# Transposing x for a small attention: TensorE transposes and a ScalarE copy, or VectorE's block transpose and DMAs

## The chip, the cores and the metric

One Trainium2 chip, one of its cores. The metric is the device time of one launch of the kernel in microseconds (us), the median of several runs. Everything is computed in float32. TensorE's clock has two levels, 1.2 and 2.4 GHz; the profile shows the granted clock as a share of the higher one.

## The reference, cut to what matters

The program is a decoder of two layers on x of 4 x 1024 x 512. Six residual blocks follow each other, each ended by a layer norm. The change lies between the last two: a cross-attention onto every sixteenth key of a context of 64 (4 keys a head, 16 heads), and a gated feed-forward on values rounded block by block.

```python
    def _L1_xattn_ref(hidden_states, key_value_states, Wq, bq, Wk, bk, Wv, bv, Wo, bo, stride):
        ...
        Q = (hidden_states @ Wq.T + bq).reshape(B, Tq, H, D).transpose(0, 2, 1, 3)
        ...
        scores = jnp.einsum('bhqd,bhkd->bhqk', Q, Kg) * scaling
        attn = jax.nn.softmax(scores, axis=-1)
        out = jnp.einsum('bhqk,bhkd->bhqd', attn, Vg)
    ...
        gate = fp4_linear(x, w_gate)
        y = fp4_linear(x, w_up)
        h = jax.nn.silu(gate) * y
        return fp4_linear(h, w_down)
```

## The kernel before, in words

The last stage of the program, `attention_outputs_and_feed_forward`, takes x as 32 tiles (`NT`) of 128 rows by 512 features. Tile n passes through these steps, each with its engine and line:

- `local_out` (TensorE, L2054): the output product of the attention before. VectorE adds it to x (`local_sum`, L2251 to L2258) and normalises the tile (`local_normal`, L2263), four slots ahead of the tile's feed-forward. Tiles 0 to 2 had this done in the stage before.
- `transpose_x` (TensorE, L2062): four 128x128 transposes of the normalised tile into one PSUM bank, `bank[SCORES]`; `copy_x` (ScalarE, L2173) copies them to `tl_XT`, of which there are two, one for even and one for odd tiles. Each 128x128 chunk lies there contiguously.
- `scores` (TensorE, L2072): four matmuls a tile, with a chunk of `tl_XT` as the stationary operand (128 columns) and 64 columns of the folded query-key weights `tl_MQ` moving. Two tiles fill one softmax.
- `shifted`, `exp`, `weights` (VectorE, ScalarE, VectorE): the softmax of both tiles. `transpose_weights` (L2078) and `attend` (L2086) are TensorE's again.
- `attended_sum`, `attended_normal`, `x_quant` (VectorE): the residual, the norm and the rounding. `xq_turned` (L2381) is VectorE's transpose in blocks of 32x32; `xq_moved` then moves the 16 blocks of 32x128 from `tl_QB` to `tl_XQT` with 16 DMAs, 8 from SyncE's queue and 8 from ScalarE's (`blocks_moved`, L1986).
- `gate_and_up` (TensorE, L2099 and L2104), in three pieces of 512, 512 and 384 columns, with `tl_XQT` stationary; `silu` (ScalarE, L2179), `product` and the rounding of h (VectorE, L2341 to L2375), `h_turned` (L2385) and `h_moved` (again 8 + 8 DMAs), `down` (TensorE, L2116, 11 matmuls), `out_sum` and `out_normal` (VectorE, L2233 to L2245) and the store (SyncE, L2020).

In `tl_XQT` and `tl_HT` the elements of a chunk do not lie side by side: `chunk(x, c)` reads every fourth (or every eleventh) float of a partition. In `tl_XT` and in the operands of L2054 and L2137 they do lie side by side.

Each engine's program is a loop over slots s = -2 to 34. Slot s does gate and up of tile s, down of tile s-1, the store of tile s-2, and `local_out` of tile s+4. In even slots the pair of tiles s+2 and s+3 passes through `transpose_x`, `scores` and the softmax (`pair(s)`). Each engine and each DMA queue works strictly in the order written, with waits on semaphores in between. A matmul in float32 shows in the trace as two records, each with its own weight load: four matmuls are 8 records. Slots -1 and 0 are the filling.

Of the kernel before, what the change touches and what calls it, by code (L numbers as in the profile page):

```python
# [10 lines left out]
ACT = mybir.ActivationFunctionType  # L11
AX = mybir.AxisListType

P = 128
B = 4
T = 1024
D = 512
C = D // P
# [40 lines left out]
class Kernel:  # L59
# [25 lines left out]
    def sb(self, ctx, name, shape, dt=F32):  # L85
        return ctx.enter_context(self.nc.sbuf_tensor(name, shape, dt))
# [26 lines left out]
    def x_tile(self, b, g):  # L113
        return self.X[:, bass.ds(b * G * D + g * D, D)]
# [90 lines left out]
EARLY = 3  # L205
# [1704 lines left out]
def attention_outputs_and_feed_forward(k):  # L1910


    a, bank = k.a, k.bank
    HM = H * KPH
    NT = B * G
    DOWN, VOUT, LOUT, SCORES = 3, (4, 5), 6, 7
    QUANT = 9
    with ExitStack() as ctx:
        sb = lambda n, s, dt=F32: k.sb(ctx, "tl_" + n, s, dt)
        sem = lambda n: k.tick("tl_" + n)  # L1920
# [22 lines left out]
        s_fq, s_ft, s_fc = (sem(n) for n in ("first_xq", "first_xqT_mm", "first_xqT"))  # L1943

        assert 2 * HM == P and B % 2 == 0
        XT, PT, SM = [sb(f"XT{p}", [P, C, P]) for p in range(2)], sb("PT", [P, P]), sb("SM", [P, 2 * HM])
        mx, sm, rc = (sb(n, [P, 2 * H]) for n in ("mx", "sm", "rc"))
        st4, mv4, ve4, rs4 = sb("st4", [P, 6]), [sb(f"mv4{p}", [P, 2]) for p in range(2)], sb("ve4", [P, 1]), sb("rs4", [P, 1])
        st5, mv5, ve5, rs5 = sb("st5", [P, 6]), [sb(f"mv5{p}", [P, 2]) for p in range(2)], sb("ve5", [P, 1]), sb("rs5", [P, 1])
# [2 lines left out]


        XB, XQB = sb("XB", [P, D]), sb("QB", [P, D])
        tmp = sb("tmp", [P, FI])

        HQ = [sb(f"HQ{p}", [P, FI]) for p in range(2)]
# [10 lines left out]
        there = lambda n: 0 <= n < NT  # L1968

        pair = lambda s: s // 2 + 1 if s % 2 == 0 and there(s + 2) else None  # L1970

        LT = NT - 1
        by_blocks = lambda n: 0 <= n < LT
# [27 lines left out]
        with k.nc.Block() as block:  # L2001
            @block.sync
            def _(e):

                def load_attended(n):
                    b, g = n % B, n // B
                    e.wait_ge(s_lo.sem, s_lo.at(n - EARLY - 1))
                    for d in k.d_ao:
                        e.wait_ge(d, 16 * B * C)
                    e.dma_start(AT[n % 2][:, :, :], k.AOd[:, b * C:(b + 1) * C, g * P:(g + 1) * P]).then_inc(s_at[n % 2].sem, 16)  # L2010

                e.dma_start(MQ[:, :], k.SW[:, M2_AT:VO_AT]).then_inc(s_wm.sem, 16)
                load_attended(EARLY)
                load_attended(EARLY + 1)

                for s in SLOTS:
                    if there(s - 2):
                        n = s - 2
                        e.wait_ge(s_x6.sem, s_x6.at(n + 1))
                        e.dma_start(k.out[n % B, (n // B) * P:(n // B + 1) * P, :], x_tile(n)).then_inc(s_out.sem, 16)  # L2020
                    if by_blocks(s - 1):
                        h_moved(e, s - 1, (0, 1))
                    if 0 < s + 1 < NT:
                        xq_moved(e, s + 1, (0, 1))
                    if EARLY + 2 <= s + 6 < NT:
                        load_attended(s + 6)
                e.wait_ge(s_out.sem, s_out.at(16 * NT))
# [21 lines left out]
            def _(e):  # L2049
# [5 lines left out]
                    mm.then_inc(s_lo.sem, 1)  # L2055

                def transpose_x(n):
                    e.wait_ge(s_x4.sem, s_x4.at(n + 1 - EARLY))
                    e.wait_ge(s_tc.sem, s_tc.at(n))
                    e.wait_ge(s_pc.sem, s_pc.at(n // 2))  # L2060
                    for c in range(C):
                        mm = e.transpose(bank[SCORES][:, c * P:(c + 1) * P], x_tile(n)[:, c * P:(c + 1) * P], k.ident[:, :])  # L2062
                    mm.then_inc(s_t.sem, 1)

                def scores(n):
                    if n == 0:
                        e.wait_ge(s_wm.sem, s_wm.at(16))

                    e.wait_ge(s_tc.sem, s_tc.at(n // 2 * 2 + 2))
                    b = n % B  # L2070
                    for c in range(C):
                        mm = e.matmul(bank[SCORES][:, HM * (n % 2):HM * (n % 2) + HM], XT[n % 2][:, c, :], M2[:, c, b * HM:(b + 1) * HM],  # L2072
                                      start=(c == 0), stop=(c == C - 1))
                    mm.then_inc(s_s.sem, 1)

# [63 lines left out]

                for s in SLOTS:  # L2140
                    j = pair(s)
                    if j is not None:
                        transpose_x(2 * j)
                    if there(s):
                        gate_and_up(s, 0)
                    if j is not None:
                        transpose_x(2 * j + 1)
                    if there(s):
                        gate_and_up(s, 1)
                    if j is not None:  # L2150
                        scores(2 * j)
                        scores(2 * j + 1)
                    if later(s + 4):
                        local_out(s + 4)
                    if there(s):
                        gate_and_up(s, 2)
                    if s + 1 == 0:
                        first_turned()
                    if j is not None:
                        transpose_weights(j)  # L2160
                    if by_blocks(s - 1):
                        down(s - 1)
                    if s - 1 == LT:
                        last_down()
                    if j is not None:
                        attend(j)

            @block.scalar
            def _(e):
                def copy_x(n):  # L2170
                    e.wait_ge(s_t.sem, s_t.at(n + 1))
                    e.wait_ge(s_s.sem, s_s.at(n - 1))
                    e.activation(XT[n % 2][:, :, :], bank[SCORES][:, :].rearrange("p (c t) -> p c t", c=C), ACT.Copy).then_inc(s_tc.sem, 1)  # L2173

                def silu(n, q):
                    x, w = PIECES[q]
                    e.wait_ge(s_g.sem, s_g.at(NP * n + q + 1))
                    e.wait_ge(s_ht.sem, s_ht.at(n - 1))
                    e.activation(HQ[n % 2][:, x:x + w], bank[(2 * q) % 3][:, 0:w], ACT.Silu).then_inc(s_sg.sem, 1)  # L2179

                def exp(j):
                    e.wait_ge(s_sx.sem, s_sx.at(j + 1))
                    e.activation(SM[:, :], SM[:, :], ACT.Exp).then_inc(s_ex.sem, 1)

                def copy_weights(j):
                    e.wait_ge(s_pm.sem, s_pm.at(j + 1))
                    e.wait_ge(s_v.sem, s_v.at(2 * j))
                    e.activation(PT[:, :], bank[SCORES][:, P:2 * P], ACT.Copy).then_inc(s_pc.sem, 1)

                def first_copied():  # L2190
                    e.wait_ge(s_ft.sem, s_ft.at(1))
                    e.activation(XQT[0][:, :].rearrange("p (t c) -> p c t", t=P), bank[DOWN][:, :].rearrange("p (c t) -> p c t", c=C),
                                 ACT.Copy).then_inc(s_fc.sem, 1)

                def last_copied():
                    e.wait_ge(s_hd.sem, s_hd.at(256 * LT))
                    for n, (x, w) in enumerate(PIECES):
                        e.wait_ge(s_lt.sem, s_lt.at(n + 1))
                        e.activation(HLT[:, x:x + w], bank[n][:, 0:w], ACT.Copy).then_inc(s_lc.sem, 1)

                for s in SLOTS:
                    j = pair(s)
                    if j is not None:
                        copy_x(2 * j)
                    if there(s):
                        silu(s, 0)
                    if s + 1 == 0:
                        first_copied()
                    elif s in FILLING:
                        xq_moved(e, s + 1, (2, 3))  # L2210
                    if j is not None:
                        copy_x(2 * j + 1)
                    if there(s):
                        silu(s, 1)
                    if by_blocks(s - 1):
                        h_moved(e, s - 1, (2, 3))
                    if j is not None:
                        exp(j)
                    if there(s):
                        silu(s, 2)  # L2220
                    if s == LT:
                        last_copied()
                    if j is not None:
                        copy_weights(j)
                    if there(s + 1) and s not in FILLING:
                        xq_moved(e, s + 1, (2, 3))

            @block.vector
            def _(e):
# [30 lines left out]
                def local_normal(n):  # L2260
                    y = x_tile(n)
                    e.wait_ge(s_r4.sem, s_r4.at(n + 1 - EARLY))
                    e.tensor_scalar(y, y, mv4[n % 2][:, 0:1], rs4[:, :], ALU.subtract, ALU.mult).then_inc(s_x4.sem, 1)  # L2263

                def attended_sum(n):
                    y = x_tile(n)
# [149 lines left out]
                for s in SLOTS:  # L2416
# [40 lines left out]
                        local_normal(s + 4)  # L2457
                    if by_blocks(s):
                        h_divide(s)
                    if s == LT:  # L2460
                        last_h(2)

# [59 lines left out]
```

## Time and profile before

| | |
|---|---|
| median of 3 runs | 2683.56 us (2677.78 to 2683.57) |
| profiled execution, its own time | 2683.64 us |
| its span, first to last instruction | 2681.8 us |
| mean granted TensorE clock | 0.988 |
| last stage | from 1559 us on, 1122 us |
| its slots 2 to 27 | some 34 us each |

PE is TensorE's matmuls, PEld its weight loads, DVE VectorE, ACT ScalarE, POOL GpSimd, SP SyncE; ACTq and SPq are the DMA queues. In a row of the trace "x8" counts records, and the time in square brackets is how long the engine stood idle before it and for what. The end of a matmul record is modelled and runs past the start of the next one, so the rate of a row of matmuls is read from starts, or from the chain of waits, where pieces join without overlap.

### The profile page before, as it was taken

What the parts mean: (1) busy time and instruction counts of PE and PEld (TensorE: products, weight loads), DVE (VectorE), ACT (ScalarE), POOL (GpSimd) and SP (SyncE); (2) the same over time, 40 slices, a digit from 0 to 9 for tenths busy, and PEclk for the clock granted to TensorE, in tenths of its full rate; (3) what the DMA queues carried; (4) which work ended last, traced back from release to release, by engine and by line L of the source; (5) the groups of instructions that cost most, each with busy time, mean ns of one, the idle gap of its engine ahead of it and who ended that gap; (6) DMA issues with size and microseconds to landing.
All of it is one profiled execution on the core that took longest, in us unless ns stands there. A gap on an engine that the chain in (4) does not pass through costs nothing. (4 is left out here: it accounts for less than half of the span.)

```text
span 2681.8 us, 36822 instructions
## 1 busy us (share of the span) xinstructions
PE 2556.6 (95%) x13053; PEld 1575.2 (59%) x13053; DVE 1915.6 (71%) x3262; ACT 749.1 (28%) x1103; POOL 866.7 (32%) x900
## 2 busy tenths in 40 slices
PE   8999998999999898999988879999999999999998
PEld 4444544555555444454544447777777777777775
DVE  4788403666667436777778858888888888888886
ACT  1111223333332235666668621111110111111100
POOL 2222203555455346676767711111111111111000
PEclk9999999999999999999999979999999999999999
DMA  5444130000000143343444421111111111111111
GB/s 175 146 151 171 52 98 35 1 0 1 1 1 1 33 103 98 98 103 95 106 105 134 139 95 36 45 45 45 46 46 44 46 43 43 43 43 46 38 39 36
DMA packets 269604, 175.94 MB, mean 66 GB/s; under 512 B 104912, under 2 KB 235344, under 8 KB 268399
## 3 DMA queue, kind: packets, MB, share of 16 engines
q1 hardware_dynamic: 238742, 148.59, 19.3%
q10 hardware_dynamic: 30680, 24.98, 3.3%
q8 instruction: 107, 1.75, 0.3%
q14 instruction: 75, 0.61, 0.1%
HBM read 90.51 MB, written 52.43 MB: 53 GB/s over the span
## 5 line engine op out<-in xcount | busy, mean ns | idle before, releaser
L2099 PE MATMUL bank<-tiles,tl_XQT 128*128 128x512 f32 (+1 forms) x768 | 328.1, 570 | 0.8 <-issue 0.8
L2104 PE MATMUL bank<-tiles,tl_XQT 128*128 128x512 f32 (+1 forms) x768 | 317.9, 557 | 0.0
L2116 PE MATMUL bank<-tiles,tl_HT 128*128 128x512 f32 x682 | 304.2, 602 | 5.0 <-DMA tl_HT<-tl_tmp 5.0
L2099 PEld LDWEIGHTS bank<-tiles,tl_XQT 128*128 128x128 f32 x768 | 233.5, 310 | 72.6 <-issue 15.8
L2104 PEld LDWEIGHTS bank<-tiles,tl_XQT 128*128 128x128 f32 x768 | 236.7, 308 | 65.9 <-issue 0.5
L2116 PEld LDWEIGHTS bank<-tiles,tl_HT 128*128 128x128 f32 x682 | 219.2, 324 | 75.7 <-issue 10.9
L1403 POOL TENSOR_SCALAR_AFFINE_SELECT tiles<-tiles 128x512 f32<-128x512 f32 x256 | 182.7, 716 | 170.1 <-ACT tiles L1630 154.4
L2179 ACT ACTIVATE tl_HQ<-bank 128x512 f32<-128x512 f32 (+1 forms) x96 | 53.9, 562 | 580.4 <-PE bank L2099 545.7
L2046 POOL TENSOR_TENSOR tl_rs<-tl_ve,mhalf 128x1 f32<-128x1 f32 x29 | 15.9, 548 | 537.1 <-DVE tl_ve L2258 537.1
L1730 DVE SCALAR_TENSOR_TENSOR tiles<-tiles,bank 128x1024 f32<-128x1024 f32 (+1 forms) x128 | 141.7, 1148 | 18.8 <-PE bank L1506 18.7
L1408 POOL TENSOR_SCALAR_AFFINE_SELECT tiles<-tiles 128x512 f32<-128x512 f32 x224 | 152.6, 681 | 0.0
L2038 POOL TENSOR_TENSOR tl_rs<-tl_ve,mhalf 128x1 f32<-128x1 f32 x32 | 18.7, 584 | 402.0 <-DVE tl_ve L2240 402.0
L1630 ACT ACTIVATE tiles<-bank 128x1024 f32<-128x1024 f32 (+1 forms) x128 | 123.4, 964 | 28.2 <-PE bank L1465 28.1
L1635 ACT ACTIVATE tiles<-tiles 128x1024 f32<-128x1024 f32 (+1 forms) x128 | 124.8, 1000 | 20.0 <-DVE tiles L1730 17.0
L1555 PE MATMUL bank<-home_T,tiles 128*128 128x512 f32 x256 | 121.5, 619 | 3.5 <-ACT tiles L1664 0.9
L977 PE MATMUL bank<-space_T 128*128 128x512 f32 x256 | 118.6, 607 | 2.5 <-DVE X L1125 2.3
L1567 PE MATMUL bank<-home_odd,tiles 128*128 128x512 f32 x256 | 117.4, 601 | 0.0
L1022 PE MATMUL bank<-space_T,space_quant 128*128 128x512 f32 x256 | 115.2, 593 | 1.5 <-ACT space_quant L1079 1.5
L1012 PE MATMUL bank<-space_even,space_quant 128*128 128x512 f32 x256 | 115.3, 593 | 1.2 <-ACT space_quant L1074 1.1
L1428 POOL TENSOR_TENSOR la_rn<-la_n,mhalf 128x16 f32<-128x16 f32 x32 | 92.7, 2897 | 52.2 <-DVE la_n L1805 52.2
L2054 PE MATMUL bank<-home_T,attended_values 128*128 128x512 f32 x232 | 107.1, 605 | 0.0
L921 POOL TENSOR_TENSOR xl_SM<-xl_SM,xl_nm 128x1024 f32<-128x1024 f32 x32 | 80.0, 2499 | 78.8 <-DVE xl_SM L1090 78.8
(301 smaller groups left out, 4701.3 us busy)
## 6 DMA issues: line engine op xcount, KB each, us to landing
tl_HT<-tl_tmp SPq DMA_DIRECT2D x248, 44.0 KB, 2.0
tl_HT<-tl_tmp ACTq DMA_DIRECT2D x248, 44.0 KB, 2.0
fp_weights<-space_quant ACTq DMA_DIRECT2D x33, 256.0 KB, 2.5
X<-in_x SPq DMA_DIRECT2D x8, 1024.0 KB, 10.7
v<-tiles SPq DMA_DIRECT2D x32, 256.0 KB, 2.4
unit_g<-tiles SPq DMA_DIRECT2D x32, 256.0 KB, 2.4
unit_gT<-tiles SPq DMA_DIRECT2D x128, 64.0 KB, 2.1
la_GN<-unit_g SPq DMA_DIRECT2D x128, 64.0 KB, 2.0
```

Of the source, the lines that this page charges most:

```text
L977: mm = e.matmul(bank[turn(s, 0)][:, :], WqT[:, c, m * P:(m + 1) * P], XT[g % 2][:, c, :], start=(c == 0), stop=(c == C - 1))
L1012: mm = e.matmul(bank[turn(s, 1)][:, :], AT[:, c, :], WoT[:, c, :], start=(c == 0), stop=(c == C - 1))
L1403: return e.affine_select(out=x[:, :, 0:P], in_=x[:, :, 0:P], compare_op=ALU.is_ge, fill=fill, base=0, pattern=[[0, HC], [1, P]], channel_m ...
L1408: return e.affine_select(out=x[:, :, P:WIN], in_=x[:, :, P:WIN], compare_op=ALU.is_ge, fill=fill, base=0, pattern=[[0, HC], [-1, P]], chan ...
L1555: mm = e.matmul(bank[1][:, :], XT[m % 2][:, c, :], WgT[:, c, :], start=(c == 0), stop=(c == C - 1))
L1567: mm = e.matmul(bank[2][:, :], XT[m % 2][:, c, :], WvT[:, c, :], start=(c == 0), stop=(c == C - 1))
L1630: e.activation(TR[p % RING][:, :, 0:cols(t)], four(ARG[:, :])[:, :, 0:cols(t)], ACT.Tanh).then_inc(s_T.sem, 1)
L1635: e.activation(y, y, ACT.Exp).then_inc(s_p.sem, 1)
L1730: e.scalar_tensor_tensor(out=y, in0=y, scalar=1.0, in1=d, op0=ALU.add, op1=ALU.mult).then_inc(s_u.sem, 1)
L2099: mm = e.matmul(bank[(2 * q) % 3][:, 0:w], chunk(XQT[n % 2], c), WgT[q][:, :, c, :], start=(c == 0), stop=(c == C - 1))
L2104: mm = e.matmul(bank[(2 * q + 1) % 3][:, 0:w], chunk(XQT[n % 2], c), WuT[q][:, :, c, :], start=(c == 0), stop=(c == C - 1))
L2116: mm = e.matmul(bank[DOWN][:, :], chunk(HT, q), WdT[:, q, :], start=(q == 0), stop=(q == IC - 1))
```

## The change

From tile 2 on, TensorE's transposes of x and ScalarE's copies are gone. In their place VectorE turns the tile in blocks of 32x32 (`x4_turned`, at the end of slot s, for tile s+4) into a buffer `X4B`, and SyncE moves the 16 blocks of 32x128 to `XT` with 16 DMAs (`x4_moved`, at the start of slot s, for tile s+3). Tiles 0 and 1 are still transposed by TensorE and copied by ScalarE. `XT` has a new layout in all cases: the four chunks are interleaved, element t of chunk c at place 4t + c, so `scores` reads it with `chunk`, as `gate_and_up` reads `XQT`.

```diff
-        XT, PT, SM = [sb(f"XT{p}", [P, C, P]) for p in range(2)], sb("PT", [P, P]), sb("SM", [P, 2 * HM])
+        XT, PT, SM = [sb(f"XT{p}", [P, D]) for p in range(2)], sb("PT", [P, P]), sb("SM", [P, 2 * HM])
...
+        X4B = sb("X4B", [P, D])
+        s_x4t, d_x4 = sem("x4_turned"), [sem(f"x4T_moved{p}") for p in range(2)]
...
+        x4_by_blocks = lambda n: 2 <= n < NT
...
+                def x4_moved(n):
+                    e.wait_ge(s_x4t.sem, s_x4t.at(n - 1))
+                    e.wait_ge(s_s.sem, s_s.at(n - 1))
+                    blocks_moved(e, range(4), X4B[:, :], XT[n % 2][:, :], d_x4[n % 2])
+
                 for s in SLOTS:
+                    if x4_by_blocks(s + 3):
+                        x4_moved(s + 3)
...
                 def transpose_x(n):
-                    e.wait_ge(s_x4.sem, s_x4.at(n + 1 - EARLY))
                     e.wait_ge(s_tc.sem, s_tc.at(n))
-                    e.wait_ge(s_pc.sem, s_pc.at(n // 2))
...
-                    e.wait_ge(s_tc.sem, s_tc.at(n // 2 * 2 + 2))
+                    e.wait_ge(s_tc.sem, s_tc.at(2))
+                    e.wait_ge(s_pc.sem, s_pc.at(n // 2))
+                    e.wait_ge(d_x4[n % 2].sem, d_x4[n % 2].at(256 * (n // 2)))
                     b = n % B
                     for c in range(C):
-                        mm = e.matmul(bank[SCORES][:, HM * (n % 2):HM * (n % 2) + HM], XT[n % 2][:, c, :], M2[:, c, b * HM:(b + 1) * HM],
+                        mm = e.matmul(bank[SCORES][:, HM * (n % 2):HM * (n % 2) + HM], chunk(XT[n % 2], c), M2[:, c, b * HM:(b + 1) * HM],
                                       start=(c == 0), stop=(c == C - 1))
...
                     e.wait_ge(s_t.sem, s_t.at(n + 1))
-                    e.wait_ge(s_s.sem, s_s.at(n - 1))
-                    e.activation(XT[n % 2][:, :, :], bank[SCORES][:, :].rearrange("p (c t) -> p c t", c=C), ACT.Copy).then_inc(s_tc.sem, 1)
+                    e.activation(XT[n][:, :].rearrange("p (t c) -> p c t", c=C), bank[SCORES][:, :].rearrange("p (c t) -> p c t", c=C), ACT.Copy).then_inc(s_tc.sem, 1)
...
+                def x4_turned(n):
+                    e.wait_ge(s_x4.sem, s_x4.at(n + 1 - EARLY))
+                    e.wait_ge(d_x4[(n - 1) % 2].sem, d_x4[(n - 1) % 2].at(256 * ((n - 1) // 2)))
+                    e.transpose(X4B[:, :].rearrange("p (j r c) -> p c j r", j=4, r=32), x_tile(n)).then_inc(s_x4t.sem, 1)
...
                     if by_blocks(s):
                         h_divide(s)
+                    if x4_by_blocks(s + 4):
+                        x4_turned(s + 4)
```

On TensorE, this is one even slot before (the order of the instructions, which has no times in it): from `down` of the slot ahead to the second piece's end and the scores.

```order
1338 L2116 MATMUL bank<-tiles,tl_HT 128x512 x11
1339 L2062 MATMUL bank<-ident,X 128x128 x4
1340 L2099 MATMUL bank<-tiles,tl_XQT 128x512 x4
1341 L2104 MATMUL bank<-tiles,tl_XQT 128x512 x4
1342 L2062 MATMUL bank<-ident,X 128x128 x4
1343 L2099 MATMUL bank<-tiles,tl_XQT 128x512 x4
1344 L2104 MATMUL bank<-tiles,tl_XQT 128x512 x4
1345 L2072 MATMUL bank<-tl_MQ,tl_XT 128x64 x8
1346 L2054 MATMUL bank<-home_T,attended_values 128x512 x4
```

The same slot after the change, where L2127 is `down`, L2110 and L2115 gate and up, L2083 the scores and L2065 `local_out`.

```order
1336 L2127 MATMUL bank<-tiles,tl_HT 128x512 x11
1337 L2110 MATMUL bank<-tiles,tl_XQT 128x512 x4
1338 L2115 MATMUL bank<-tiles,tl_XQT 128x512 x4
1339 L2110 MATMUL bank<-tiles,tl_XQT 128x512 x4
1340 L2115 MATMUL bank<-tiles,tl_XQT 128x512 x4
1341 L2083 MATMUL bank<-tl_MQ,tl_XT 128x64 x8
1342 L2065 MATMUL bank<-home_T,attended_values 128x512 x4
```

Two groups of four transposes are gone; the scores are as many as before.

On SyncE's queue, one slot after the change, up to the next slot's start. Before, such a slot was the last four of its rows alone (L2020, L1986, L1986 and L2010 there).

```order
548 L1990 DMA tl_XT<-tl_X4B 32x128 x16
549 L2031 DMA out<-X 128x512
550 L1990 DMA tl_HT<-tl_tmp 32x352 x8
551 L1990 DMA tl_XQT<-tl_QB 32x128 x8
552 L2014 DMA attended_values<-attended 128x4x128
```

The 16 new DMAs stand first, ahead of the store, and every later DMA of the slot is behind them.

On VectorE, the end of a slot after the change and the start of the next: L2361 to L2369 are `h_divide`, L2278 is the new transpose, L2243 is `out_sum`.

```order
1772 L2361 TENSOR_REDUCE tl_am<-tl_HQ 128x88
1773 L2363 TENSOR_SCALAR tl_sc<-tl_am 128x88
1774 L2365 RECIPROCAL tl_rs<-tl_sc 128x88
1775 L2367 TENSOR_SCALAR tl_rs<-tl_rs 128x88
1776 L2369 TENSOR_TENSOR tl_HQ<-tl_HQ,tl_rs 128x1408
1777 L2278 STREAM_TRANSPOSE tl_X4B<-X 128x4x128
1778 L2243 TENSOR_TENSOR X<-bank,X 128x512
```

The new transpose stands between `h_divide` and the wait for `down`.

## Rows read from the trace of the kernel before

**Rows 1.** The page, busy time, share and instructions of each engine.
```profile
PE 2556.6 (95%) x13053; PEld 1575.2 (59%) x13053; DVE 1915.6 (71%) x3262; ACT 749.1 (28%) x1103; POOL 866.7 (32%) x900
```
**Rows 2.** Windows of the last stage, PE: length, busy, records, granted clock, DMA.
```profile
1601.00:1640.00 39.00, 37.63 (x113) 1.00 0.11 29
1640.00:2553.00 913.00, 913.00 (x2552) 1.00 0.16 44
```
**Rows 3.** The chain of waits, 2020 to 2100 us: start, length, what.
```profile
2027.99 3.43 PE bank L2104 x8
...
2056.32 0.44 PE bank L2062 x4
2056.76 3.55 PE bank L2099 x8
2060.31 3.43 PE bank L2104 x8
2063.75 0.44 PE bank L2062 x4
2064.18 3.56 PE bank L2099 x8
...
2071.17 1.73 PE bank L2072 x16
...
2081.77 9.58 PE bank L2116 x22
```
**Rows 4.** Weight loads by line: duration in ns, least, median, most.
```profile
L2072 PEld LDWEIGHTS bank<-tl_MQ,tl_XT x256: 186/192/333, 1563.1 to 2549.8; 128*128 128x128 f32 x128
...
L2137 PEld LDWEIGHTS bank<-tiles,tl_tmp x22: 190/190/190, 2665.5 to 2674.5; 128*128 128x128 f32 x22
...
L2099 PEld LDWEIGHTS bank<-tiles,tl_XQT x768: 307/308/332, 1583.9 to 2647.1; 128*128 128x128 f32 x192
```
**Rows 5.** Timeline from 2024.2 us, the first weight loads and the first matmul of a slot.
```profile
2024.16 0.54 PEld L2099 LDWEIGHTS bank<-tiles,tl_XQT 128*128 128x128 f32 x2 [0.33 <-issue]
2024.16 0.82 PE L2099 MATMUL bank<-tiles,tl_XQT 128*128 128x512 f32 x1
```
**Rows 6.** Groups by line from 1540 us on: count, busy, mean ns, idle before.
```profile
L2381 DVE STREAM_TRANSPOSE tl_QB<-tl_XQ 128x512 f32<-128x512 f32 x31 | 34.5, 1113 | 0.6
...
L2233 DVE TENSOR_TENSOR X<-bank,X 128x512 f32<-128x512 f32 x32 | 22.1, 692 | 113.9 <-PE bank L2116 107.5 <-PE bank L2137 6.4
...
L2078 PE MATMUL bank<-ident,tl_SM 128*128 128x128 f32 x32 | 6.7, 291 | 4.3 <-DVE tl_SM L2298 4.3
```
**Rows 7.** Timeline, the end of an odd slot and the even one after it.
```profile
2050.74 0.46 SPq L2010 DMA_DIRECT2D attended_values<-attended  x1
...
2051.12 1.63 DVE L2354 TENSOR_TENSOR tl_HQ<-tl_HQ,tl_rs 128x1408 f32<-128x1408 f32 x1
...
2067.35 0.36 SPq L2020 DMA_DIRECT2D out<-X  x1
...
2071.01 1.89 PE L2072 MATMUL bank<-tl_MQ,tl_XT 128*128 128x64 f32 x16
...
2071.61 6.32 SPq L1986 DMA_DIRECT2D tl_HT<-tl_tmp  x8
```
**Rows 8.** DMAs of tl_XQT: ns on SyncE's queue; us to landing.
```profile
L1986 SPq DMA_DIRECT2D tl_XQT<-tl_QB x248: 507/591/1572, 1595.3 to 2624.3; - x124
...
DMA to landing us min/median/max: 1.7/1.8/3.2
```
**Rows 9.** Timeline, the filling, 1562 to 1638 us.
```profile
1562.32 0.60 ACT L2173 ACTIVATE tl_XT<-bank 128x512 f32<-128x512 f32 x1 [1.22 <-PE bank L2062]
1563.08 3.49 PEld L2072 LDWEIGHTS bank<-tl_MQ,tl_XT 128*128 128x128 f32 x16 [1.20 <-DMA tl_MQ<-folded]
...
1582.73 1.07 ACT L2192 ACTIVATE tl_XQT<-bank 128x512 f32<-128x512 f32 x1 [12.46 <-PE bank L2122]
...
1601.46 1.86 PEld L2072 LDWEIGHTS bank<-tl_MQ,tl_XT 128*128 128x128 f32 x16 [0.76 <-ACT tl_XT L2173]
...
1637.43 8.10 PE L2116 MATMUL bank<-tiles,tl_HT 128*128 128x512 f32 x18 [0.96 <-DMA tl_HT<-tl_tmp]
```

More of the change, by code:

```diff
@@ L2141, in _ @@
                     j = pair(s)
-                    if j is not None:
-                        transpose_x(2 * j)
+                    if j == 0:
+                        transpose_x(0)
                     if there(s):
                         gate_and_up(s, 0)
-                    if j is not None:
-                        transpose_x(2 * j + 1)
+                    if j == 0:
+                        transpose_x(1)
                     if there(s):
@@ L2202, in _ @@
                     j = pair(s)
-                    if j is not None:
-                        copy_x(2 * j)
+                    if j == 0:
+                        copy_x(0)
                     if there(s):
@@ L2210, in _ @@
                         xq_moved(e, s + 1, (2, 3))
-                    if j is not None:
-                        copy_x(2 * j + 1)
+                    if j == 0:
+                        copy_x(1)
                     if there(s):
```

## The prediction

> **What bounds the kernel now.** I read the shares by engine first: TensorE is busy 95% of the span and VectorE 71% [rows 1]. A share is a mean over stages, so the windows of the last stage come next. From 1640 to 2553 us TensorE is busy for all 913 of 913 us, at the full granted clock of 1.00 (2.4 GHz) [rows 2]. All pairs of tiles but the first two lie there, so in this stretch time is what TensorE's queue takes, end to end, and nothing else counts unless it makes TensorE wait. The chain of waits says the same: piece joins piece, all on PE [rows 3]. It also gives the true cost of each group, since its pieces do not overlap.
>
> **What is removed.** A group of four transposes is 0.44 us in the chain [rows 3]. It costs more than that: the group of L2099 behind it takes 3.55 to 3.56 us, where L2104, with the same eight loads and 512 columns but no transposes ahead, takes 3.43 [rows 3]. Behind a short matmul the first load of the group is not covered. So a group is worth 0.44 + 0.12 = 0.56 us. There are 30 (tiles 2 to 31). That of tile 2 stands in the filling, where TensorE waits anyway for the first rounded tile, which ScalarE's copy [rows 9] brings; I count 29, which gives 29 x 0.56 = 16.2 us. In slot 0 the scores waited 0.76 us for ScalarE's copy of tile 3 [rows 9], held up behind its DMA issues. That copy is gone: 0.8 us more. Together **-17.0 us**. The other copies were waited for by nobody: ScalarE is idle most of the time [rows 1], and their going is worth nothing.
>
> **What is changed without being named: the weight load of the scores.** The scores' eight matmuls a pair show as 16 records with 64 moving columns, 1.73 us in the chain, which is 0.108 us a record [rows 3]. What is the limit of such a record? Matmuls with 512 columns go at 3.43 / 8 = 0.429 us; at that rate 64 columns would stream in 0.054 us. So the 0.108 are not the stream; they are the load. Now the layout: the loads of the scores read side by side and last 192 ns, as those of L2137 (190 ns). The loads of L2099 read every fourth float, and last 308 ns, the least of 768 being 307 [rows 4]. A duration holds a fixed part, but the difference of 118 ns is not in the fixed part, as the start of a slot shows: two such loads last 0.54 us together [rows 5], so the second starts 0.54 - 0.31 = 0.23 us after the first (0.01 us is the rounding); and the first matmul of that group is recorded with 0.82 us, where its median is 0.59. Adding the difference to the present rate gives 0.108 + 0.118 = 0.226. Behind 512 columns a load of 0.22 us is covered by the 0.43 us of streaming, which is why it costs L2099 nothing today. Behind 64 columns nothing covers it.
>
> The trace of before has no row with strided loads and a short stream, so this is the disputed price. From below: nothing, 0.108 us a record as now. From above: each load in full after the other, 0.308 us. I take 0.222, nearest to the spacing read off [rows 5] and a hair below the sum of 0.226, because this spacing is the one measurement in which one such load follows another with no stream between. That is 16 x (0.222 - 0.108) = 1.83 us a pair. There are 16 pairs. The first runs at the lower clock, where 16 loads side by side took 3.49 us already, 0.22 us each [rows 9]; a strided load can be no faster there, and I let it cost nothing more. 15 x 1.83 = **+27.4 us**. The bounds are 0 and 15 x 16 x 0.200 = 48 us.
>
> The Trainium skill, in SBUF — State Buffer, "Specifications (TRN2)", says that SBUF has 16-byte cachelines and that each access that crosses to a new line pays a penalty, with at least two hits a line needed for full bandwidth. Every fourth float is a new line each time; the 308 against 192 ns [rows 4] agree with it. It has no size for it. The Trainium skill, in TensorE: Matmul & The Clock Gate, "LDWEIGHTS (loading the stationary operand)", makes the load's time the number of columns over 1.2 alone. By it 128 columns take 107 ns in either layout, which is the 0.108 us of today; the scores would cost what they cost, and the whole would come out at the time of the first rival below. The rows of L2099 speak against it.
>
> **What is added on VectorE.** x4_turned is the twin of xq_turned, the same tile size with the same interleaved writing, 1113 ns [rows 6]. It stands at the end of the slot. Behind it VectorE waits for `down` in every slot: 113.9 us over 32 tiles, 3.6 us a slot [rows 6]. 1.1 us fit in that hole and leave over 2 us, so it costs nothing in slots 2 on; without the hole it would be 28 x 1.1 = 31 us. In the filling there is no such hole. In slot 1 TensorE waits 0.96 us for h of tile 0 [rows 9], VectorE being the one that is late; the transpose for tile 4 stands right ahead of that work. **+1.1 us**.
>
> **What is added on SyncE.** 16 DMAs of 32x128, like those of tl_XQT, at a median of 0.591 us of issue [rows 8]: 9.5 us a slot. Take the slot in [rows 7]. h_divide ends at 2051.12 + 1.63 = 2052.75, the transpose at 2053.9; SyncE has been free since 2051.2. Issues end at 2063.4, the last lands 1.8 us later (3.2 at worst) [rows 8], at 2065.2 to 2066.6. The scores want it at 2071.0, or 2069.9 once both groups of transposes are gone. Slack 3 to 5 us. What is queued behind: the store at 2067.35 and h_moved at 2071.61, both still waiting for VectorE when the queue is free again at 2063.4. xq_moved and load_attended come later still. So **0**, hidden behind 14 us of gate and up. The wait for the former scores on the same XT is long met, and the wait of x4_turned for the move of the tile before too. The softmax starts at the end of the scores and shifts with them, and so do local_out and the third piece on TensorE, so the 4.3 us that TensorE waits for it in all (L2078) [rows 6] stay.
>
> **Tiles 0 and 1.** ScalarE's copies now write every fourth float. The one copy of this kind took 1.07 us at 1582.73 against 0.60 for the present one [rows 9]. Both copies stand in series ahead of the first scores: 0.94 us, of which some is covered by the DMA that the scores wait for anyway (1563.08, while the copy ended at 1562.92). **+0.9 us** with rounding.
>
> **Sum.** -17.0 + 27.4 + 1.1 + 0.9 = +12.4 us. The profiled execution took 2683.64 us (span 2681.8 and 1.8 around it), 0.08 above the median of 2683.56, so the forecast is **2696 us**. 0.3% is 8 us; it is about what a measurement can tell from no change, and the bounds for it are 2675.5 and 2691.6.
>
> **The rivals.**
>
> 1. *The stride costs nothing in the scores* (faster). For: the records of gate and up go at 0.429 us with strided loads, as fast as any others. Against: [rows 4, 5]. Then -17.0 + 2.0 = -15.0, **2669 us**. It is decided at the spacing of two loads: 15.0 us over 240 records is 0.063, so below 0.108 + 0.063 = 0.170 us a load the change gains, above it loses. 0.10.
> 2. *Part of the stride is absorbed*, 0.13 to 0.20 us a load. Then 2674 to 2691 us. Nothing in the rows asks for it, except that the spacing is read at one place and rounded. 0.10.
> 3. *Loads in series*, 0.308 us each, when each waits for the matmul that uses the one before: +48 instead of +27.4, **2717 us**. Against: today a record of 0.108 us is shorter than its load of 192 ns, so loads overlap in their fixed part. 0.05.
> 4. *SyncE is late with tile s+3.* If issues took over 0.9 us each (some have 1.57 [rows 8]), the last would land after 2070, and TensorE would wait in each even slot; at 1.2 us an issue, 2053.9 + 19.2 + 1.8 = 2074.9, some 3 us beyond the first tile's scores, 15 times: +45, **2741 us**. Against: the median of 0.59. 0.05.
> 5. *VectorE's transpose reaches TensorE.* In odd slots VectorE has the least room. If 0.5 us of it came through in 28 slots, +14, **2710 us**. 0.03.
>
> The forecast itself has 0.67, with a load of 0.205 to 0.235 us: 2692 to 2700.
>
> **How the numbers follow.** Case 1 and part of case 2 are faster by 0.3%: 0.12. Most of case 2 and the foot of the forecast are within 0.3%: 0.14. The rest is slower: 0.74. The range for 8 in 10 takes in the forecast and the upper half of case 2 below, and some hidden cost on VectorE or SyncE above: 2684 to 2706.
>
> **What would show each step.** In the profile after: the scores' loads at 308 ns, not 192, and the scores of a pair in the chain at 3.5 us, not 1.73; the group of L2099 behind the slot's start at 3.43 instead of 3.55; no rows of transposes beyond the first eight; TensorE busy throughout 1640 to 2560; an even slot longer by some 0.7 us and an odd one unchanged; VectorE's wait for `down` shorter by 1.1 us a slot; no wait of the scores for the DMAs; the wait for h of tile 0 at about 2 us. I am wrong if the scores of a pair stay below 2.8 us (rivals 1 and 2), or if they wait (rival 4).

## The result, and the profile after

The kernel after takes 2703.24 us (median, 2696.64 to 2705.15), the one before 2683.11 (2677.78 to 2683.57): a ratio of 1.0075, with a 95% interval of 1.0054 to 1.0097. It is slower by 20 us. In a second set of runs the ratio was 1.0081 (1.0068 to 1.0095). The forecast was 2696 us, between 2684 and 2706. The profiled execution happens to be the fastest, 2696.64 us with a span of 2694.9; what sets it apart from the others is taken up near the end.

The chain of waits of the kernel after, one even slot, answers to [rows 3]. L2110 and L2115 are gate and up, L2083 the scores, L2065 `local_out`, L2127 `down`.

```profile
2063.77 3.43 PE bank L2110 x8
2067.20 3.43 PE bank L2115 x8
2070.63 3.43 PE bank L2110 x8
2074.07 3.43 PE bank L2115 x8
2077.50 3.55 PE bank L2083 x16
2081.05 3.49 PE bank L2065 x8
...
2089.92 9.57 PE bank L2127 x22
```

The slot starts with gate; both groups of transposes are gone, and both groups of L2110 are at 3.43 us. The scores took 1.73 us; they take 3.55. The weight loads of the scores, line by line as in [rows 4]:

```profile
L2083 PEld LDWEIGHTS bank<-tl_MQ,tl_XT x256: 307/329/332, 1560.3 to 2566.2; 128*128 128x128 f32 x128
```

They last 307 ns or more, as those of gate always did, and no longer 192. The length of a pair of slots, an even one and an odd one, is read off the starts of the same group in neighbouring pairs. First the kernel before, in the chain of waits from 1640 us on:

```profile
1800.18 3.49 PE bank L2054 x8
...
1868.36 3.49 PE bank L2054 x8
```

Then the kernel after, in the same view:

```profile
1729.68 3.55 PE bank L2083 x16
...
1798.57 3.55 PE bank L2083 x16
...
1867.45 3.55 PE bank L2083 x16
1871.00 5.18 PE bank L2065 x8
...
1938.03 3.55 PE bank L2083 x16
```

Before, a pair of slots takes 68.18 us. After, it takes 68.88 or 68.89: +0.70, which is 1.82 for the loads less 1.12 for two groups of transposes. The last pair shown takes 70.58. There `local_out`, with the same eight records, takes 5.18 us in place of 3.49. The windows say why:

```profile
2000.00:2010.00 10.00, 10.00 (x32) 1.00 0.11 38
2010.00:2020.00 10.00, 10.00 (x25) 0.83 0.27 69
2080.00:2090.00 10.00, 10.00 (x32) 1.00 0.28 72
2566.00:2576.00 10.00, 9.85 (x26) 0.83 0.23 58
```

In each row stand the window, its length, TensorE's busy time with its records, the granted clock and two numbers on the DMAs. Behind the scores at 2006.92 the clock is 0.83 over ten microseconds; that is 3.4 us at the lower of its two levels (1.2 GHz) and the rest at 2.4, so 1.7 us are lost. Before the fall TensorE had done 3.55 us of the scores. From tile 2 on, 14 pairs have a `local_out` behind their scores; in the profiled execution the clock falls behind 4 of them. The last pair has no `local_out`; a fifth fall stands behind its scores (the last row above), but it costs nothing: TensorE waits for the softmax there, 1.85 us before and 0.15 us now, and from the end of the scores to the transposing of the weights it is 7.17 us in both kernels. The kernel before has no fall behind its scores.

One more fall stands in the filling, behind TensorE's wait for h of tile 0. It is read from the first `down`, in the kernel before and after:

```profile
1637.43 9.82 PE bank L2116 x22
...
1635.84 11.23 PE bank L2127 x22
```

VectorE and SyncE, the parts that were forecast at nothing in these slots, from the end of the slot ahead of the first chain above to the scores of that chain:

```profile
2060.11 1.10 DVE L2278 STREAM_TRANSPOSE tl_X4B<-X 128x512 f32<-128x512 f32 x1
2061.24 10.01 SPq L1990 DMA_DIRECT2D tl_XT<-tl_X4B  x16
2074.80 0.36 SPq L2031 DMA_DIRECT2D out<-X  x1
2076.91 3.31 PEld L2083 LDWEIGHTS bank<-tl_MQ,tl_XT 128*128 128x128 f32 x13
```

The 16 DMAs are issued by 2071.3 and land 1.8 us later (median of all), 3.8 us ahead of the first load of the scores. SyncE is free 3.5 us before the store's turn. From 1640 to 2560 us no matmul waits for a DMA, as before. VectorE's wait for `down` fell from 86.5 to 68.4 us over 27 slots, 0.7 us a slot; 1.1 had been expected.

### The profile page after: what moved, and what is told of

It is laid out like the page before. It is cut to its first block and busy times, and to the rows that moved or that the text cites. A ratio compares the mean times of both kernels' runs of the same rounds, so it can differ in the third digit from the quotient of the medians.

```text
span 2694.9 us, 37090 instructions
## 1 busy us (share of the span) xinstructions
PE 2568.6 (95%) x12933; PEld 1594.0 (59%) x12933; DVE 1945.3 (72%) x3292; ACT 733.3 (27%) x1073; POOL 867.0 (32%) x900
## 5 line engine op out<-in xcount | busy, mean ns | idle before, releaser
L2110 PE MATMUL bank<-tiles,tl_XQT 128*128 128x512 f32 (+1 forms) x768 | 324.7, 566 | 1.2 <-issue 1.2
L2115 PE MATMUL bank<-tiles,tl_XQT 128*128 128x512 f32 (+1 forms) x768 | 318.0, 557 | 0.0
L2127 PE MATMUL bank<-tiles,tl_HT 128*128 128x512 f32 x682 | 302.2, 599 | 6.4 <-DMA tl_HT<-tl_tmp 6.4
L2110 PEld LDWEIGHTS bank<-tiles,tl_XQT 128*128 128x128 f32 x768 | 235.7, 309 | 79.9 <-issue 16.0
L2115 PEld LDWEIGHTS bank<-tiles,tl_XQT 128*128 128x128 f32 x768 | 236.8, 308 | 66.0 <-issue 0.5
L2127 PEld LDWEIGHTS bank<-tiles,tl_HT 128*128 128x128 f32 x682 | 219.2, 324 | 75.2 <-issue 10.1
L2065 PE MATMUL bank<-home_T,attended_values 128*128 128x512 f32 x232 | 114.0, 638 | 0.0
```

The lines of the kernel that those rows point to most:

```text
L2065: mm = e.matmul(bank[LOUT][:, :], AT[n % 2][:, c, :], WoT[:, c, :], start=(c == 0), stop=(c == C - 1))
L2110: mm = e.matmul(bank[(2 * q) % 3][:, 0:w], chunk(XQT[n % 2], c), WgT[q][:, :, c, :], start=(c == 0), stop=(c == C - 1))
L2115: mm = e.matmul(bank[(2 * q + 1) % 3][:, 0:w], chunk(XQT[n % 2], c), WuT[q][:, :, c, :], start=(c == 0), stop=(c == C - 1))
L2127: mm = e.matmul(bank[DOWN][:, :], chunk(HT, q), WdT[:, q, :], start=(q == 0), stop=(q == IC - 1))
```

## The experiments

All times are medians of device time; each ratio is to the kernel before on the same chip.

**The layout alone.** The kernel before, transposes and copies kept, with XT interleaved:

```diff
-                    e.activation(XT[n % 2][:, :, :], bank[SCORES]...
+                    e.activation(XT[n % 2][:, :].rearrange("p (t c) -> p c t", c=C), bank[SCORES]...
...
-                        mm = e.matmul(..., XT[n % 2][:, c, :], M2[...]
+                        mm = e.matmul(..., chunk(XT[n % 2], c), M2[...]
```

> The kernel before with one edit: ScalarE's copy writes XT with the four chunks interleaved and the scores read every fourth float; transposes and copies stay for all tiles. Theory of the load: the scores of a pair go from 1.73 to 3.55 us in the chain of waits, 15 times, +27 us, and the granted clock may fall behind some of them, 1.7 us each, up to 15 times: 2710 to 2736 us, with the loads of the scores at 308 ns. Rival (the stride costs nothing in itself; what the change lost lies in VectorE's or SyncE's new work): 2683 us within 0.3%.

Measured: 2731.78 us, 1.0183 (1.0169 to 1.0197): +49 us from a layout, with no new work. The chain of waits of this kernel, where L2062 are the transposes, L2072 the scores and L2054 `local_out`:

```profile
2086.05 0.43 PE bank L2062 x4
2086.49 3.56 PE bank L2099 x8
2090.04 3.43 PE bank L2104 x8
2093.48 3.56 PE bank L2072 x16
2097.03 5.18 PE bank L2054 x8
```

The scores are at 3.56 us, and of the 14 groups of `local_out` behind scores from 1600 to 2640 us only 2 are at 3.49, while 12 are at 4.96 to 5.19. 15 x 1.82 = 27.3 and 12 x 1.7 = 20.4 make 47.7; the last stage, from the load of `tl_MQ` to the end, is 1170.3 us of this profile and 1122.6 of the one before, 47.7 more. That the two agree to the tenth is luck: smaller terms, such as the longer copies ahead of the first scores and one fall fewer near the end, cancel. The rival is out.

**The change with side-by-side chunks.** VectorE writes its blocks chunk by chunk, the 16 DMAs move 128-byte runs, four to a partition, in place of one of 512. `XT` and ScalarE's two copies have the layout of the kernel before:

```diff
-                    blocks_moved(e, range(4), X4B[:, :], XT[n % 2][:, :], d_x4[n % 2])
+                    for i in range(4):
+                        for j in range(4):
+                            e.dma_start(XT[n % 2][32 * j:32 * j + 32, :, 32 * i:32 * i + 32],
+                                        X4B[32 * i:32 * i + 32, P * j:P * j + P].rearrange("p (c r) -> p c r", c=C)).then_inc(d_x4[n % 2].sem, 16)
...
-                        mm = e.matmul(..., chunk(XT[n % 2], c), M2[...]
+                        mm = e.matmul(..., XT[n % 2][:, c, :], M2[...]
...
-                    e.transpose(X4B[:, :].rearrange("p (j r c) -> p c j r", j=4, r=32), x_tile(n)).then_inc(s_x4t.sem, 1)
+                    e.transpose(X4B[:, :].rearrange("p (j c r) -> p c j r", j=4, c=C), x_tile(n)).then_inc(s_x4t.sem, 1)
```

> The kernel after, but each chunk of XT lies side by side: VectorE writes its blocks in the order of chunks, and SyncE's 16 DMAs move 128-byte runs in place of 512-byte ones. Theory of the load: the scores are back at 1.73 us a pair, the 30 groups of transposes stay gone: 2683 - 17 + 2 = 2668 us, granted clock back at 0.988 or above. Rival (the new work on VectorE or SyncE is what costs): no faster than the kernel after, 2697 to 2705 us. If the shorter runs make the DMAs late, the scores show a wait for DMAs in even slots, which either theory allows.

Measured: 2665.04 us, 0.9936 (0.9923 to 0.9948). It beats both kernels: 18 us below before, 38 below after. Its chain of waits, where L2086 are the scores and L2068 `local_out`:

```profile
2056.42 3.43 PE bank L2118 x8
2059.85 1.73 PE bank L2086 x16
2061.58 3.49 PE bank L2068 x8
```

and the rows of XT and X4B:

```profile
L2025 SPq DMA_DIRECT2D tl_XT<-tl_X4B x480: 591/601/1405, 1567.5 to 2522.3; - x160
L2281 DVE STREAM_TRANSPOSE tl_X4B<-X x30: 703/705/711, 1566.8 to 2511.9; 128x512 f32<-128x512 f32 x30
```

The scores are back at 1.73. The shorter runs cost SyncE 601 ns an issue in place of 591. No fall of the clock behind the scores.

**The scores of the two tiles apart.** The kernel after with one edit on TensorE:

```diff
+                    if j is not None:
+                        scores(2 * j)
                     if there(s):
                         gate_and_up(s, 1)
                     if j is not None:
-                        scores(2 * j)
                         scores(2 * j + 1)
```

> The kernel after, with the scores of the two tiles of a pair apart: the even tile's four matmuls ahead of the second piece of gate and up, the odd tile's behind it. The same loads, in two stretches of 1.8 us in place of one of 3.55. Theory that the long stretch of short matmuls lets the granted clock fall: no falls behind the scores, L2065 at 3.49 us in all even slots, 2693 to 2697 us against some 2703. It also exposes the first strided load of a group once more, +0.12 us a pair, 2 us in all. Rival (the 7 us between the profiled run and the other runs of the kernel after have another cause): 2703 us plus 2.

Measured: 2698.16 us (2696.95 to 2700.30), 1.0058 (1.0045 to 1.0070), some 5 us below the kernel after and a microsecond above the 2693 to 2697 us of its theory. The chain of waits:

```profile
2005.44 1.69 PE bank L2083 x8
2007.12 3.61 PE bank L2110 x8
2010.73 3.43 PE bank L2115 x8
2014.17 1.69 PE bank L2083 x8
2015.85 3.49 PE bank L2065 x8
```

1.69 + 1.69 + 3.61 is 6.99 us, as 3.55 + 3.43 is 6.98: the loads cost the same. But `local_out` is at 3.49 in all 14 even slots. The falls behind the scores are gone, and with them 5 us. It is not the whole 6.8 of four falls: this profile has falls elsewhere, two of which the first profile of the kernel after lacks (`down` at 2574.56 us takes 11.29 us and at 2638.51 us 11.53, in place of 9.6 and 9.8).

**What the change removes, priced alone.** The kernel before, without the transposes and copies from tile 2 on:

```diff
-                    if j is not None:
-                        transpose_x(2 * j)
+                    if j == 0:
+                        transpose_x(0)
```

and so for the second tile of the pair and for `copy_x`; the scores wait for the first two copies only.

> The kernel before, without TensorE's transposes and ScalarE's copies from tile 2 on and with nothing in their place: the scores of tiles 2 to 31 read what tiles 0 and 1 left in XT, so this part of the computation is left out. It prices what the change removes. Forecast of the sum: 16.2 + 0.8 us, 2683 - 17 = 2666 us. Rival (transposes are partly covered, 0.44 us a group or less): 2670 us or more. If 2668 for the kernel with chunks side by side and the new moves is right as well, the two differ by what the new work costs, 2 us.

Measured: 2666.11 us, 0.9938 (0.9925 to 0.9952): 16.7 us for the transposes, with 17 forecast. The complete side-by-side kernel is at 2665.04, so what VectorE's transposes and SyncE's DMAs cost TensorE is too small for this comparison, whose intervals are each 3 to 4 us wide.

**The same, with every fourth float.** The edits of the layout alone on the kernel just above.

> As the kernel without transposes and with nothing in their place, but XT is interleaved and read with every fourth float: the computation of the scores of tiles 2 to 31 is left out in part as there. Theory of the load: 2666 + 27.4 + up to 15 falls of the granted clock of 1.7 us: 2693 to 2718 us; the difference to the kernel after (some 2703 us) is what VectorE's transposes and SyncE's DMAs cost, expected within 4 us. Rival (the new work is what costs): near 2666 us.

Measured: 2699.88 us, 1.0072 (1.0059 to 1.0085). Against the 0.9938 with chunks side by side that is 0.0134 of 2683, or 36 us, for the layout: 27.3 for the loads and 4 falls of 1.7 us seen in its profile, 34 in all. The four falls lie 208.35 us apart, three pairs each:

```profile
2011.82 5.18 PE bank L2054 x8
```

Beside the kernel with the layout alone, this one lacks TensorE's transposes and ScalarE's copies from tile 2 on, with the waits that belong to them, and nothing else. So with the transposes 12 groups of `local_out` are slow, and without them 4.

**The kernel after once more.**

> The kernel after, unchanged, beside the others on one chip. If the falls of the granted clock behind the scores explain the spread of its runs (2696.64 to 2705.15), its median is again near 2703 us and its spread wider than that of the kernel with the scores apart (2696.95 to 2700.30).

Measured: 2703.53 us (2701.06 to 2704.35), 1.0081 (1.0068 to 1.0095). The median holds. The spread is 3.3 us, as that with the scores apart, so that half of the expectation failed: the odd one is the first profiled run alone. This profile has 5 falls behind the scores, against 4 there, and some elsewhere.

**Every second float.** The kernel without the transposes once more, with the chunks interleaved in pairs (ScalarE's copy writes them so):

```diff
+        by_pairs = lambda x, c: x[:, :].rearrange("p (a t b) -> p a b t", a=2, b=2)[:, c // 2, c % 2, :]
...
-                        mm = e.matmul(..., XT[n % 2][:, c, :], M2[...]
+                        mm = e.matmul(..., by_pairs(XT[n % 2], c), M2[...]
```

> As the one with every fourth float and nothing in place of the transposes, but the chunks are interleaved in pairs, so that a load reads every second float, two in each 16 bytes. If two hits in 16 bytes are enough for a load at full rate, the scores take 1.73 us a pair and the time is 2666 us. If any stride halves the rate, 3.55 us a pair and the time of the kernel with every fourth float. In between if the price goes by the bytes passed over.

Measured: 2667.98 us, 0.9948 (0.9935 to 0.9962). The load's row:

```profile
L2074 PEld LDWEIGHTS bank<-tl_MQ,tl_XT x256: 195/196/332, 1561.7 to 2534.4; 128*128 128x128 f32 x128
```

196 ns, against 192 side by side and 307 or more with every fourth. In the chain of waits the scores of a pair take 1.82 us, against 1.73 and 3.55. A stride as such costs next to nothing. Then the complete kernel with this layout, moved in 256-byte runs:

> The kernel after, complete, with the chunks of XT interleaved in pairs and moved in 256-byte runs, read with every second float. If a load with every second float costs 196 against 192 ns, as in the run that left the transposes out, the time is that of the side-by-side kernel, 2665 to 2668 us; no falls of the clock behind the scores. A kernel for which DMAs of 128-byte runs would be too many would take this one.

Measured: 2668.05 us, 0.9946 (0.9933 to 0.9960), no falls behind the scores.

**Side by side for gate and up too.** `xq_moved` in 128-byte runs and `XQT` read in chunks of 128.

> The kernel with side-by-side XT, and XQT laid out side by side as well (VectorE writes its blocks in order, the same DMAs move 128-byte runs). Its loads are covered by 512 columns except the first of a group behind a short matmul: the group of gate behind attend goes from 3.75 us to 3.63 or less in each even slot, 16 times 0.12 = 2 us; VectorE's transpose of XQ falls from 1.11 to 0.70 us, which TensorE does not wait for. Forecast 2663 us against 2665.04. Rival (the load's stride matters for covered loads too, through the 0.43 us a record): over 10 us faster.

Measured: 2667.51 us, 0.9948 (0.9935 to 0.9960). No gain in the median, where 2 us were forecast and the intervals of both are 3 us wide; the rival's 10 are out. The chains of waits are finer. First the group of gate behind `attend` in the side-by-side kernel, then here:

```profile
2014.03 3.75 PE bank L2113 x8
...
2017.40 3.63 PE bank L2119 x8
```

The 0.12 us is there, and a pair takes 66.94 us in place of 67.06. Over the stage that is under 2 us, and one more fall of the clock in this profile (`down` at 2541.89 us takes 11.29 us) takes as much back. All other groups of gate and up take what they took: loads behind 512 columns are covered at 308 ns.

**The scores twice, with fast loads.** The side-by-side kernel with

```diff
-                    for c in range(C):
+                    for c in 2 * list(range(C)):
```

> The kernel with side-by-side XT, each tile's four matmuls of the scores done twice (the second time from zero, so the scores are the same): 32 records of 0.108 us, a stretch of 3.46 us as long as that of the strided loads (3.55), but full of twice as many matmuls. Price of the doubling: 15 x 1.73 + 1.7 at the low clock = 28 to 30 us on 2665. Theory A, the granted clock falls because a long stretch consists of short matmuls: falls behind the scores as in the kernel after or more, 4 to 12 of 1.7 us, 2700 to 2715 us. Theory B, it falls because TensorE stands still while the strided loads trickle in: no falls, 2692 to 2696 us.

Measured: 2697.21 us, 1.0052 (1.0039 to 1.0065), a microsecond above theory B and 3 below theory A. Its chain of waits:

```profile
2010.43 3.52 PE bank L2086 x32
2013.95 3.49 PE bank L2068 x8
```

A stretch as long as the slow scores, full of matmuls, and `local_out` is at 3.49 in all 14 even slots. The falls behind the scores come with the slow loads, not with the length of a stretch of short matmuls; theory A is out. That TensorE stands still between the loads, as theory B has it, is argued and not shown.

## Why the prediction was right, and where it was short

**The removal.** 29 groups of 0.56 us and 0.8 us in slot 0 made 17.0; the run that does this alone gives 16.7. That a group is worth more than its own 0.44 us, because the load behind it is not covered, holds: L2110 at the slot's start went from 3.55 to 3.43.

**The strided load.** Forecast at 0.222 us a record and 3.55 us a pair, measured at 3.55 or 3.56. The reading of two loads that follow each other at a slot's start [rows 5] carried the whole forecast: one place, read to 0.01 us. The sign hung on it: the side-by-side kernel shows what rival 1 would have been, 2665 us against the 2669 forecast for it. The Trainium skill's rule on 16-byte lines (SBUF — State Buffer, "Specifications (TRN2)") is borne out by the row with every second float: two hits in a line, and the load goes at 196 ns. The Trainium skill's formula in "LDWEIGHTS (loading the stationary operand)" of TensorE: Matmul & The Clock Gate, which knows only the number of columns, gives 107 ns for either layout. It fits the 0.108 us of a record with chunks side by side, and the 0.222 us of a record with every fourth float contradicts it.

**The new work.** VectorE's transpose took 1.10 us as forecast, and behind it VectorE's wait for `down` had room for it; SyncE's issues took 10.0 us where 9.5 were forecast. The transpose in slot 1 reached TensorE: the wait for h of tile 0, 0.96 us before [rows 9], is 2.4 now, where 2.1 was forecast. That the rest costs nothing from 1640 us on is shown by the pair of slots, 67.1 us both in the side-by-side kernel and in the one with no new work at all.

**The first pair.** At the lower clock the strided loads were taken to cost nothing. The 16 loads took 3.81 us against 3.49 [rows 9]: 0.3 us too little. The copies of tiles 0 and 1 were priced at 0.9 us. Each took 1.07 us, as forecast, but from the load of `tl_MQ` to the first scores it is 4.15 us in the first profile and 4.60 in the second, against 3.89 before: 0.3 and 0.7 us.

**What was missing.** The sum had no term for the clock; nothing in it or in the rivals let the slower loads lower the granted clock. Of the 20 us between the medians 12.4 were in the sum. The rest is explained by the second profile, whose time of 2704.35 us is near the median: from the load of `tl_MQ` to the end it takes 1143.7 us, against 1122.6 of the kernel before, 21.0 more. To the 12.4 come 8.2 for five falls behind the scores and 1.7 for the one behind the wait for h of tile 0 (`down` takes 11.51 us there, 9.82 before); a fall near the end that the kernel before has, at 2620 us, is missing, less 1.7. That makes 20.6.

**What was luck.** The first profiled execution met the forecast of 2696 although it has such falls too. Its last stage takes 16.1 us more than that of the kernel before: 12.4, with 6.8 for four falls and 1.4 for the one behind the wait for h, less 3.4 for two falls near the end of the kernel before (behind 2616 and 2656 us) that are not in it, and a rest of -1.1. The stage also began 3.0 us earlier (`tl_MQ` loaded at 1556.17 against 1559.19). So the agreement to 1 us is luck; that of the pair of slots (0.70 us more, where 0.7 was forecast) is not. The median of 2703 lies above the 2692 to 2700 that the forecast gave to its own case. It is inside the range because that was widened up to 2706 for hidden cost on VectorE or SyncE; that cost did not come, and the clock took its place.

**What stays open.** Why only 4 or 5 of 14 slow groups of scores are followed by a fall in the kernel after, and 12 of 14 with the transposes kept. That it is due to the transposes and copies is shown, by one profile of each kernel: the one with every fourth float and no transposes has 4. The medians agree, 30 us apart, which is 16.7 for the transposes and 13.6 for eight falls. But they do two things: they put short matmuls into the slot, and they lengthen the pair, from 68.9 to 70.0 us where no fall comes in, so that the scores start at other moments. The falls come at regular distances: in the kernel after some 139 or 208 us, which is two or three pairs, and with the transposes kept 71.7 us, every pair, from 1810 us on. This speaks for the moments at which the scores start, but no run shifted them alone. Nor did a run test why the clock falls behind the wait for h of tile 0. TensorE waited 2.4 and 2.3 us there in the two profiles of the kernel after, which have the fall, and 2.05 us in the side-by-side kernel and 0.96 in the kernel before, which do not.

## What to carry to other kernels

A layout change that removes work on the engine that bounds the kernel must be costed at its reader too: interleaved float32 chunks, read as the stationary operand with every fourth element, double the weight load (0.22 for 0.11 us a record). Here that was free behind 512 moving columns, but for the first load of a group behind a short matmul (0.12 us), and full price behind 64. Before such a change, look in the trace for two loads that follow each other with no stream between; their spacing is what a record with few moving columns will take. Where a block transpose is moved by DMA anyway, let the DMA leave the chunks side by side, or in pairs of elements: both of these versions gained (2665 and 2668 us) where the one with every fourth float lost. And a forecast to a few microseconds needs a term for the clock wherever the change slows a stretch of loads.

## What the runs showed of the hardware that had not been expected

- TensorE's granted clock fell to the lower level for 3.4 us behind stretches of 3.55 us of slow weight loads (4 or 5 of 14, with the transposes kept 12 of 14), and behind none of 14 when the stretch was cut in two of 1.69 us, or was as long but filled with 32 records in place of 16.
- VectorE's block transpose of 128x512 float32 took 1.103 us when it wrote every fourth float and 0.705 us when it wrote runs of 32 side by side.
- At the lower clock, 16 loads with every fourth float took 3.81 us and 16 side by side 3.49; at the higher clock 3.55 and 1.73.
- SyncE issued a DMA of 128 runs of 128 bytes in 601 ns and one of 32 runs of 512 bytes in 591 ns; both landed 1.8 us later.
